# Head norms of a random-feature attention stage, computed as exp(0.5 ln(x)) instead of with the square-root function

## The reference, cut to what matters

```python
def _feature_map(x, rf):
    proj = jnp.einsum('bhnd,fd->bhnf', x, rf) / jnp.sqrt(jnp.float32(NUM_FEATURES))
    norm = jnp.linalg.norm(x, axis=-1, keepdims=True)
    return jnp.exp(proj - norm)
...
q_prime = _feature_map(q, random_features)
k_prime = _feature_map(k, random_features)
kv = jnp.einsum('bhnf,bhnd->bhfd', k_prime, v)
normalizer = jnp.einsum('bhnf,bhf->bhn', q_prime, k_prime.sum(axis=2))
out = jnp.einsum('bhnf,bhfd->bhnd', q_prime, kv)
out = out / (normalizer[..., None] + 1e-06)
...
x = x + _layernorm(_L0_attn_ref(_layernorm(x, axis=-1), ...), axis=-1)
x = x + _layernorm(_L0_ffn_ref(_layernorm(x, axis=-1), ...), axis=-1)
```

## Time and profile before

| | |
|---|---|
| median of 3 runs | 1995.95 us (1994.59 to 1996.98) |
| the profiled execution | 1997.2 us, its span in the trace 1995.4 us |
| TensorE matmul busy | 1785.7 us, 89% of the span |
| VectorE busy | 1388.3 us, 70% |
| ScalarE busy | 1291.6 us, 65% |
| GpSimd busy | 1208.3 us, 61% |
| mean granted TensorE clock | 0.981 of full speed |

### The profile page before, as it was taken

One profiled execution on the slowest core, in us unless ns is written; L12 is line 12 of the kernel. 1 busy time (PEld: TensorE's weight loads), 2 busy tenths in 40 slices (PEclk: granted clock), 3 DMA queues, 4 the chain that ended last, 5 costly groups with the idle time before them and its releaser, 6 DMA issues.

```text
span 1995.4 us, 54188 instructions
## 1 busy us (share of the span) xinstructions
PE 1785.7 (89%) x18756; PEld 1224.4 (61%) x18884; DVE 1388.3 (70%) x3157; ACT 1291.6 (65%) x2692; POOL 1208.3 (61%) x1143
## 2 busy tenths in 40 slices
PE   4999999689999999999969988999999999996997
PEld 3666666456666666666645655666666666664554
DVE  3777777667777777777757756777777776774897
ACT  4878888457777777777742216777777777774221
POOL 0323233277777777777743217777777777774464
PEclk9999999889999999999999998999999999999999
DMA  4211111211111111111113321111111111111343
GB/s 100 55 49 46 50 45 48 56 29 37 33 34 32 34 32 39 35 32 34 30 39 91 91 59 29 37 33 34 32 34 32 39 35 32 34 30 45 97 126 90
DMA packets 209334, 94.31 MB, mean 47 GB/s; under 512 B 90818, under 2 KB 200300, under 8 KB 209260
## 3 DMA queue, kind: packets, MB, share of 16 engines
q1 hardware_dynamic: 209260, 93.35, 17.9%
HBM read 51.03 MB, written 25.23 MB: 38 GB/s over the span
## 4 chain that ended last, share of the span: by engine, by line
PE 66%; ACT 17%; issue 10%; DVE 3%; POOL 1%; DMA 1%; SPq 1%; ACTq 1%; POOLq 0%; DVEq 0%
PE banks L926 17%; ACT pr L769 8%; PE banks L976 5%; PE banks L946 5%; PE banks L1250 5%; PE banks L1263 4%; PE banks L1253 4%; ACT kT L800 4%; PE banks L1005 4%; PE banks L561 3%; PE banks L510 3%; PE banks L1042 3%; PE banks L575 3%; PE banks L1024 2%; PE banks L1034 2%
## 5 line engine op out<-in xcount | busy, mean ns | idle before, releaser
L663 POOL TENSOR_TENSOR m2q<-qraw,ltab 128x256 f32<-128x256 f32 x256 | 244.6, 975 | 251.3 <-ACT qraw L779 229.3
L722 POOL TENSOR_TENSOR rr<-ss,half_neg 128x16 f32<-128x16 f32 x128 | 374.5, 2925 | 19.1 <-POOL ss L719 17.0
L769 ACT ACTIVATE pr<-banks,nb,rr 128x128 f32<-128x128 f32 x1024 | 372.7, 478 | 0.8 <-DVE nb L900 0.8
L926 PE MATMUL banks<-ident,pr 128*128 128x128 f32 x1024 | 161.3, 280 | 60.1 <-ACT pr L769 57.5
L1166 ACT ACTIVATE f_g<-banks,b_s 128x512 f32<-128x512 f32 (+1 forms) x96 | 65.9, 686 | 200.5 <-PE banks L1250 192.3
L888 DVE TENSOR_REDUCE ss<-sq 128x16 f32<-128x1024 f32 x128 | 156.1, 1220 | 31.0 <-ACT sq L809 28.1
L1006 PE MATMUL banks<-vt,pT 128*64 128x65 f32 x2048 | 173.9, 228 | 0.0
L962 PEld LDWEIGHTS banks<-wo_s,oT 128*128 128x128 f32 x1024 | 134.0, 191 | 63.3 <-issue 45.9
L745 ACT COPY hT<-banks 128x128 f32<-128x128 f32 x128 | 34.1, 267 | 213.9 <-PE banks L940 213.9
L733 POOL TENSOR_TENSOR qrot<-m1q,m2q 128x512 f32<-128x512 f32 x128 | 163.0, 1273 | 14.2 <-POOL m1q L668 8.2
L926 PEld LDWEIGHTS banks<-ident,pr 128*128 128x128 f32 x1024 | 113.6, 141 | 86.5 <-ACT pr L769 86.5
(11 more groups left out here) (130 smaller groups left out, 4648.2 us busy)
## 6 DMA issues: line engine op xcount, KB each, us to landing
ve<-vt SPq DMA_DIRECT2D x128, 130.0 KB, 2.2
hs<-y_d SPq DMA_DIRECT2D x128, 64.0 KB, 1.9
yt<-y_d SPq DMA_DIRECT2D x64, 128.0 KB, 2.1
y_d<-yn SPq DMA_DIRECT2D x64, 128.0 KB, 2.0
f_h<-y_d SPq DMA_DIRECT2D x128, 64.0 KB, 2.0
f_y<-y_d SPq DMA_DIRECT2D x64, 128.0 KB, 2.2
xa<-in_L_attn_x SPq DMA_DIRECT2D x32, 128.0 KB, 2.1
xr<-in_L_attn_x SPq DMA_DIRECT2D x32, 128.0 KB, 2.3
```

The source lines that it names most:

```text
L663: m = on.tensor_tensor(d4[:, :, c, :], s4[:, :, 1 - c, :], sin, ALU.mult)
L722: nc.gpsimd.tensor_tensor(rr[:, r, :], ss[:, r, :], half_neg[:], ALU.pow).then_inc(T["rr"], 1)
L769: a = nc.scalar.activation(pr[:, e, j, :], bank[e][:, j * P:(j + 1) * P], ACT.Exp, bias=nb[:, X.t, UH * e + j:UH * e + j + 1], scale=rr[:, ...
L926: m = nc.tensor.transpose(b[:, j * P:(j + 1) * P], src[:, j * P:(j + 1) * P], ident[:])
```

## The change

The square root of the sums of squares is replaced by two ScalarE instructions: the natural logarithm of the sum plus 2^-64 (added as a bias operand, one value per partition, held in the new tile `a_tiny`), written to the new tile `a_ln`; and the exponential of half of that, written to `nrm`. The logarithm signals a new semaphore `A["ln"]`; the exponential waits for it. The logarithm also waits for the `nrm` of the sequence before, which guards `a_ln`. The exponential of one column in front of the `kf` exponentials is taken out. GpSimd fills `a_tiny` in the setup.

```diff
-            nc.gpsimd.memset(half_neg[:], -0.5).then_inc(set_c, 1)
+            nc.gpsimd.memset(half_neg[:], -0.5)
+            nc.gpsimd.memset(a_tiny[:], 2.0 ** -64).then_inc(set_c, 1)
...
-        a_exp = sa("a_exp", [P, 1])
+        a_ln = sa("a_ln", [P, 2 * N])
...
             if on.now:
                 act.wait_ge(A["ss_ps"], i + 1)
-                nc.scalar.activation(nrm[:, p].rearrange("p a n -> p (a n)"), bank[4][:], ACT.Sqrt
+                until(act, A["nrm"], i)
+                nc.scalar.activation(a_ln[:], bank[4][:], ACT.Ln, bias=a_tiny[:, 0:1]).then_inc(A["ln"], 1)
+                act.wait_ge(A["ln"], i + 1)
+                nc.scalar.activation(nrm[:, p].rearrange("p a n -> p (a n)"), a_ln[:], ACT.Exp, scale=0.5
                                      ).then_inc(A["nrm"], 1)
...
             if on.now:
-                nc.scalar.activation(a_exp[:], half_neg[:, 0:1], ACT.Exp)
                 act.wait_ge(A["kf_ps"], i + 1)
```

More of the change, by code:

```diff
@@ L111, in build @@
         half_neg = sb("half_neg", [P, 16])
+        a_tiny = sb("a_tiny", [P, 1])
         tabs = sb("tabs", [P, 4, TPB, DH])
```

## The result

| | before | changed |
|---|---|---|
| median | 1995.68 us (4 runs, 1994.59 to 1996.98) | 2095.64 us (4 runs, 2092.52 to 2097.53) |
| ratio of the times | | 1.0497, 95% interval 1.0481 to 1.0514 |
| span of the profiled execution | 1995.4 us | 2093.1 us |
| stage A ends: first copy of stage T on ScalarE | 397.4 us | 499.3 us |

The change makes the kernel 5.0% slower. The forecast was 3.2% slower, with 2060.0 us; the measured time lies 36 us above it and outside the range of 1984 to 2065. All of the loss lies in stage A: it ends 101.9 us later, and what follows takes 1593.8 us in place of 1598.0.

A forecast was written before the change was run, and what follows sets the result against it. TensorE and ScalarE looked nearly level in stage A, with TensorE waiting for `nrm`. Two loads in front of `nrm` cost 31 x 2.02 = 62.6 us plus 1.5 in the first sequence: +64.1, 2060.0 us, range 1984 to 2065.

The forecast's parts named there:

- a later `nrm` is paid in full: Stage A: TensorE's L561 already waits for `nrm` in 31 sequences, so 2.02 us later costs 31 x 2.02 = 62.6 us.
- the handover: ScalarE, logarithm to exponential: a wait of the engine for itself, taken as 0.04 us, with 0.15 as the other end.
- the load in front of the `a_exp` exponential: At L484, before `kf`: the 1.28 us load is off the path, so taking it out gains no time.
- what is to be seen at the first load: ScalarE at 22.77 us: tables look chosen one instruction at a time, without regard to the next function.
- longest-run rule: Skill's rule that the compiler places loads greedily by longest run; with the ln/exp set, it implied no load per sequence.
- The first rival: Stage A: one table holds logarithm and exponential, no loads in the sequence; 1986.5 us, 1984 to 1989.5, chance 0.25.
- the clock: Rival in stage A: two loads and a lower TensorE clock, longer matmuls, time above 2066 us; chance 0.03.
- the two loads: Likeliest case, stage A: loads before logarithm and exponential, both in front of `nrm`; 2060.0 us, 2056 to 2064, chance 0.66.

The follow-up runs named there:

- one-table kernel: Changed kernel plus one instruction loading, before stage A, the table that holds logarithm and exponential together; 1987.47 us, ratio to before 0.9951.
- filling: Changed kernel plus seven 128x128 matmuls with unread results, on TensorE in the pause for `nrm`; 2064.13 us, ratio to before 1.0340.
- one-load kernel: Changed kernel with the exponential making `nrm` replaced by square, so the second load moves to in front of `kf`; 2021.35 us, ratio to before 1.0117.
- two copies: Kernel before plus two 128x512 ScalarE copies with unread results, in front of the square root's load; 2026.94 us, ratio to before 1.0156.
- three copies: Kernel before plus three 128x512 ScalarE copies with unread results, in front of the square root's load; 2073.04 us, ratio to before 1.0392.

## Why the prediction was wrong

The direction, the mechanism and its price held; one step failed and carried 37 us.

- **Right: a later `nrm` is paid in full.** Both loads stand in front of `nrm`, the stretch from `qf` to `nrm` grew by 2.04 us (2.02 forecast), and the logarithm took 0.687 us (0.69). Two small terms were off and nearly cancel: the exponential took 0.63 and not 0.60, and the handover of 0.04 us, which the one-table kernel shows, is not paid in the changed kernel, where the load starts 0.01 us behind the logarithm and covers it. With TensorE's clock held up by filling, the total was 2064.1, against 2060.0 forecast and 3.1 + 1.7 us that the filling itself and the last sequence account for.
- **Right: the load in front of the `a_exp` exponential was worth nothing.** In the one-load kernel, where one stands in front of `kf`, ScalarE still waits 0.31 us for TensorE behind it.
- **Right: what is to be seen at the first load.** The loads are where a choice made one function at a time puts them: two in each sequence of exponential, logarithm, exponential. One earlier load of a table with both functions removed every load of the stage. The Trainium skill's page "ScalarE: Activation LUTs", section "Table sets: the hidden batching unit", has one load for ln followed by exp; the one-table kernel agrees, the changed kernel, with 64 loads in 32 sequences, does not. The longest-run rule of the Trainium skill's page "ScalarE activation tables: per-element evaluation and per-set limits", section "Table sets in the compiler and the runtime", does not describe the loads of these kernels.
- **The first rival: right in its mechanism, its number in part by luck.** 1986.5 was forecast for no loads in the sequence, 1987.5 measured once the table was given. The forecast had 9 us from 30 sequences at 0.30 and 0.4 from the first two; the run showed 8.0 from the sequences, at 0.26, and 1.5 from the first load, which the load placed by hand took out of the way and which the rival had not counted.
- **Wrong: the clock.** The forecast put the new period at 12.96 us with TensorE 82% busy, took a stretch of 10 us that was 76% busy at a clock of 1.00, and gave a fall of the clock 0.03. It failed in what was compared. One row of 10 us at the end of the stage, with idle time that came in several pieces (the three longest are below), was made to answer for 32 pauses of 2.2 us in one piece each. The runs show what it could not: two copies, with pauses of 1.0 to 1.2 us, kept the clock at 1.00, and 0.5 us more in each pause brought it to 0.92. The trace of before had a row of the right kind too: the first matmuls of the stage, where TensorE still waited on and off, were slower than later ones of the same shape (L561 of the first sequence begins with 0.93 us for eight matmuls where 0.71 is usual); it was read only for its start time. The pieces of the earlier trace rows:

```profile
376.07 0.71 PE L519 MATMUL banks<-wT,a_oT 128*128 128x128 f32 x4 [0.59 <-DVE a_oT L590]
...
378.53 0.44 PE L545 MATMUL banks<-ident,a_kvT 128*128 128x128 f32 x2 [0.74 <-DVE a_kvT L616]
379.79 1.93 PE L575 MATMUL banks<-qf,kvb 128*32 128x256 f32 x32 [0.82 <-DVE kvb L623]
```

- **The range.** It was built of the two loads and the one table, and its upper end took the likeliest case with 5 us on top. The clock stood in the text as a rival without a price. With the clock at half for L561 alone, the price was there to be worked out from the earlier trace rows: 31 x 2.0 = 62 us if every sequence is hit; 37 were lost.

What stays open: why one pause is followed by a slow spell and the next, as long, is not. In the four sequences shown of the changed kernel the pauses of 2.27 and 2.25 us were not hit and those of 2.18 and 2.17 were; with three copies the hit ones come in uneven groups, and the two-copy kernel's pauses of 1.78 and 1.65 at the start were not hit. The rows show which, not why.

## What to carry to other kernels

Where a function is replaced by two others, count the table loads by where they stand, not by how many there are: here 64 stayed 64, and 32 of them moved from beside the path onto it. If the functions fit one table, load that table once by hand ahead of the loop, and look in the trace that no load is left. And price a new wait of TensorE twice, once for its length and once for the work behind it at half clock, as soon as it is one unbroken pause longer than the 1.2 us that cost no clock here; look at how long the pauses are, and not only at the busy share.

## What the runs showed of the hardware

- Pauses of TensorE of up to 1.2 us in a loop with a period of 11 to 13 us left the granted clock at 1.00; with 1.5 to 1.7 us it was 0.92, with 2.0 to 2.3 us 0.90 to 0.93, and the slow matmuls came right behind a pause or up to 1.0 us after its end. This held with table loads, with copies, with the old function and the new.
- Matmuls whose result nobody reads, put into a pause that is there anyway, made a kernel 31.5 us faster (ratios to before 1.0340 and 1.0497).
- A ScalarE instruction that waits for the one right before it starts 0.03 to 0.04 us after its end, as in one of VectorE's two cases.
- A table load stood for 1.28 us between two instructions with 0.01 to 0.02 us on either side, and in front of an instruction that waited for TensorE it cost nothing.
- An exponential of 128x512 with its input in SBUF took 0.630 us and a square root of the same shape from PSUM 0.597.
